# Cross-attention of a decoder layer on one core: batches written out, values copied by ScalarE, their bias added to the heads

## What is computed

```
# query = layernorm(x), (32, 100, 256); key_value = ctx, (32, 361, 192); 16 heads of 16 channels
q = (query @ Wq + bq)   ; k = (key_value @ Wk + bk)   ; v = (key_value @ Wv + bv)   # split into heads
attn = clip(einsum('bhqd,bhkd->bhqk', q, k) * D ** -0.5, -1e4, 1e4)
attn = softmax(attn, axis=-1)
x = einsum('bhqk,bhkd->bqhd', attn, v).reshape(B, Nq, Cq)
return x @ Wo + bo
```

## Time and profile before

| what | value |
|---|---|
| median of three runs | 1663.99 us (1661.3 to 1667.15) |
| the profiled execution | 1657.89 us |
| its span, first to last instruction | 1656.1 us |
| TensorE matmuls busy | 1392.7 us, 84% |
| TensorE weight loads | 973.8 us, 59% |
| VectorE busy | 1054.5 us, 64% |
| ScalarE busy | 516.9 us, 31% |
| GpSimd busy | 785.4 us, 47% |
| mean granted clock of TensorE | 0.926 |

### The profile page before, as it was taken

The page is one execution under the profiler, slowest core; times in us unless marked ns, Lnnn a source line. Parts: engine busy times, 40 slices in busy tenths (PEclk is TensorE's granted clock), DMA queues, the critical chain, the costliest instruction groups (busy, mean ns, idle before and its releaser), DMA issues. The chain is left out here.

```text
span 1656.1 us, 33994 instructions
## 1 busy us (share of the span) xinstructions
PE 1392.7 (84%) x9914; PEld 973.8 (59%) x9915; DVE 1054.5 (64%) x2457; ACT 516.9 (31%) x1228; POOL 785.4 (47%) x1072
## 2 busy tenths in 40 slices
PE   4788778877745998989898898989998499999997
PEld 2556545555533776767676676666765266666664
DVE  2687897788731688868788787878886222222221
ACT  1333323332301334434344343434442122222221
POOL 4233552355332457757576576657774122222222
PEclk9899999999875799989899998999996699999999
DMA  4991000000004545545555454555652122222222
GB/s 144 316 319 31 1 1 1 0 0 1 1 12 84 73 91 108 117 90 111 104 106 109 76 115 103 109 101 102 116 109 62 41 46 45 45 45 45 45 46 25
DMA packets 180315, 128.11 MB, mean 77 GB/s; under 512 B 68882, under 2 KB 173090, under 8 KB 180194
## 3 DMA queue, kind: packets, MB, share of 16 engines
q1 hardware_dynamic: 167890, 112.36, 31.2%
q0 software_dynamic: 12304, 14.10, 5.6%
HBM read 36.23 MB, written 44.83 MB: 49 GB/s over the span
## 5 line engine op out<-in xcount | busy, mean ns | idle before, releaser
L1323 DVE TENSOR_REDUCE neg_raw<-bank_s 100x2 f32<-100x722 f32 x256 | 231.1, 903 | 102.2 <-PE bank_s L1539 102.2
L1225 ACT ACTIVATE prob<-bank_st 120x400 f32<-120x400 f32 (+1 forms) x384 | 166.0, 506 | 270.6 <-PE bank_st L1556 270.6
L1880 POOL DMA_INDIRECT out<-result,target x57 | 88.2, 1547 | 266.9 <-DVE result L1854 263.7
L1334 DVE TENSOR_SCALAR bank_st<-bank_st 120x400 f32<-120x400 f32 (+1 forms) x384 | 196.6, 572 | 0.0
L1539 PE MATMUL bank_s<-k_st,q_st 96*100 96x361 bf16 x512 | 137.3, 352 | 55.7 <-issue 20.7
L1080 POOL TENSOR_TENSOR neg_diag<-xident_b,neg_max 100x400 bf16<-100x400 bf16 x128 | 109.2, 853 | 149.9 <-DVE neg_max L1328 140.9
L748 PE MATMUL bank_l<-q_heads,k 128*100 128x192 f32 (+4 forms) x512 | 126.9, 390 | 62.0 <-DVE attn L562 49.8
L1865 DVE TENSOR_TENSOR hidden<-silu,ebank_v 128x512 f32<-128x512 f32 x57 | 39.2, 687 | 196.1 <-PE ebank_v L1789 196.1
L748 PEld LDWEIGHTS bank_l<-q_heads,k 128*100 128x100 f32 x512 | 82.9, 180 | 112.9 <-DVE attn L562 43.5
L396 ACT ACTIVATE q_heads<-q 32x192 f32<-32x192 f32 (+3 forms) x168 | 62.1, 370 | 226.2 <-DVE q L521 217.8
L1547 PEld LDWEIGHTS bank_st<-q_st,k_st 96*120 96x120 bf16 (+1 forms) x1536 | 117.7, 143 | 12.8 <-ACT prob L1225 0.5
(11 more groups left out here) (203 smaller groups left out, 2688.9 us busy)
## 6 DMA issues: line engine op xcount, KB each, us to landing
k_st<-k_part SPq DMA_DIRECT2D x384, 90.2 KB
slot_rows<-empty SPq DMA_DIRECT2D x9, 2967.0 KB, 26.1
q_st<-q_part SPq DMA_DIRECT2D x384, 25.0 KB
kv<-in_ctx_t SPq DMA_DIRECT2D x32, 270.8 KB
expert_w<-in_w SPq DMA_DIRECT2D x16, 512.0 KB, 3.9
rows<-slot_rows SPq DMA_DIRECT2D x57, 129.0 KB, 2.0
residual<-in_w SPq DMA_DIRECT2D x16, 256.0 KB, 4.1
residual<-in_x SPq DMA_DIRECT2D x8, 400.0 KB
```

The lines of the kernel that those rows point to most:

```text
L1225: act.activation(prob[0:KEYS[c], t % 2, c], bank_st[c][0:KEYS[c], 0:4 * T], ACT.Exp).then_inc(exp_done, 1)
L1323: dve.tensor_reduce(neg_raw[:, h:h + 2], bank_s[0:T, :, 0:S], AX.X, ALU.max, negate=True).then_inc(max_done, 1)
L1334: dve.tensor_scalar(tile, tile, CLAMP, -CLAMP, ALU.min, ALU.max).then_inc(clipped, 1)
```

## The change

Three things. `every_batch` calls `body` for all 32 batches with plain numbers; the counted loop of the attention stage is gone on all five engines. `values`, which moves the value matmuls' results from bank_v to `val`, is now a ScalarE copy without a bias: at t = 0 parts 0 and 1 stand behind `out_copy` and ahead of `exps`, at t = 1 part 2 stands ahead of `heads_turn`. And the bias bv is added where ScalarE copies the turned heads: there the channels lie on partitions, so the bias is one column for each half, and the one copy of 200 columns becomes two instructions of 100 columns with a bias. `out_project` waits for both.

```diff
-def every_batch(eng, body):
-
-    for b in range(4):
-        body(b, b, 0)
-    with eng.Fori(1, BATCH // 4 - 1) as i:
-        for q in range(4):
-            body(4 * i + q, q, i)
-    for b in range(BATCH - 4, BATCH):
-        body(b, b % 4, BATCH // 4 - 1)
+def every_batch(body):
+
+    for b in range(BATCH):
+        body(b, b % 4, b // 4)
...
-        b_v = sb("xb_v", [128, D])
+        b_v = sb("xb_v", [128, CC])
...
             def heads_turn(b):
+
                 act.wait_ge(heads_turned, b + 1)
-                act.activation(heads_t[:], bank_m[:, 0:CC * T].rearrange("p (c t) -> p c t", c=CC),
-                               ACT.Copy).then_inc(heads_t_done, 1)
+                for c in range(CC):
+                    act.activation(heads_t[:, c], bank_m[:, c * T:(c + 1) * T], ACT.Identity,
+                                   bias=b_v[:, c:c + 1]).then_inc(heads_t_done, 1)
+
+            def values(b, p, c):
+                act.wait_ge(v_summed, 3 * b + max(c + 1, 2))
+                act.activation(val[0:KEYS[c], p, c, 0:17 * NH].rearrange("p (h d) -> p h d", d=17)[:, :, 0:16],
+                               bank_v[0:KEYS[c], (c % 2) * D:(c % 2 + 1) * D].rearrange("p (h d) -> p h d", d=16),
+                               ACT.Copy).then_inc(v_done, 1)
...
                 queries(b)
+                if b == 0:
+                    for c in range(3):
+                        values(0, 0, c)
...
                 for t in range(4):
+                    if t == 1 and more_than(b, 1):
+                        values(b + 1, 1 - q % 2, 2)
                     if t == 1 and not first:
                         heads_turn(b - 1)
...
                     if t == 0 and not first:
                         out_copy(b - 1)
+                    if t == 0 and more_than(b, 1):
+                        values(b + 1, 1 - q % 2, 0)
+                        values(b + 1, 1 - q % 2, 1)
...
-            def values(b, p, c):
-                dve.wait_ge(v_summed, 3 * b + max(c + 1, 2))
-                dve.tensor_tensor(val[0:KEYS[c], p, c, 0:17 * NH].rearrange("p (h d) -> p h d", d=17)[:, :, 0:16],
-                                  bank_v[0:KEYS[c], (c % 2) * D:(c % 2 + 1) * D].rearrange("p (h d) -> p h d", d=16),
-                                  b_v[0:KEYS[c], :].rearrange("p (h d) -> p h d", d=16),
-                                  ALU.add).then_inc(v_done, 1)
...
-            for c in range(3):
-                values(0, 0, c)
...
-                    if t == 0 and more:
-                        values(b + 1, 1 - p, 0)
-                        values(b + 1, 1 - p, 1)
-                    if t == 1 and more:
-                        values(b + 1, 1 - p, 2)
...
-                pe.wait_ge(heads_t_done, b + 1)
+                pe.wait_ge(heads_t_done, CC * (b + 1))
...
-        "xbv": np.broadcast_to(a["bv"], (128, D)), "xbo": np.broadcast_to(a["bo"], (T, D)),
+        "xbv": a["bv"].reshape(CC, 128).T, "xbo": np.broadcast_to(a["bo"], (T, D)),
```

More of the change, by code:

```diff
@@ L1020, in body @@
                         load_w2(n - 2)
-            every_batch(sp, body)
+            every_batch(body)
             keep(BATCH - 2)
@@ L1173, in body @@
                     diag(b + 1, 0)
-            every_batch(pool, body)
+            every_batch(body)
             last = BATCH // 2 - 1
@@ L1285, in body @@
                         keys_high(b + 2, t - 2)
-            every_batch(act, body)
+            every_batch(body)
             out_copy(BATCH - 1)
@@ L1471, in body @@
                         negated(n + 1, (t + 1) % 4)
-                    if t == 0 and more:
-                        values(b + 1, 1 - p, 0)
-                        values(b + 1, 1 - p, 1)
-                    if t == 1 and more:
-                        values(b + 1, 1 - p, 2)
-            every_batch(dve, body)
+            every_batch(body)
             last = BATCH // 2 - 1
@@ L1683, in body @@
                             count(2 * i - 1 + q // 2, x_done, b)
-            every_batch(pe, body)
+            every_batch(body)
             last = BATCH // 2 - 1
```

## The result

The changed kernel takes 1612.72 us (median of four runs, 1610.59 to 1614.91); the kernel before took 1665.57 us beside it. The ratio is 0.9675, with a 95% interval of 0.9629 to 0.972: faster by 47 to 62 us. A later comparison on another chip gave 0.9729 (0.9696 to 0.9762), 40 to 51 us. The forecast was 1632 us, 32 us less, with a range that ended at 1616. The side and the main cause were right, the size was some 20 us too small.

A forecast was written before the change was run, and what follows sets the result against it. TensorE, busiest at 84%, was taken to lose time at the attention loop's jumps. Terms -35.9 - 2.8 + 8.1 - 1.0 = -31.6, say -32 us, from 1663.99 gave 1632 us, range 1616 to 1648.

The forecast's parts named there:

- The loop: Attention stage, batches 7 to 24: writing out the counted loop removes five jumps back, 35.9 us saved.
- The wait with "issue": TensorE before a batch's first scores, once per jump back: 20.7 us in all; none over 2.5 us expected after.
- the clock stayed at 1.00: Sign of being right: granted clock 1.00 in every attention pair, with pairs of 43 to 44 us.
- no wait at the pace of the instruction blocks: Gaps at the pace of 16 KB instruction fetches in the attention stage would have shown the prediction wrong.
- The starved rival: Written-out attention code waits for late instruction blocks, up to 1821 us if all 47 are late; chance 0.04.
- VectorE's relief: 96 value additions leave VectorE in the attention batches, 37.6 us of work, almost none on the path: 2.8 us saved.
- The 0.2 us in even batches: Router's MAX8 starts earlier once VectorE's additions go, in 14 even batches with a `place`: 2.8 us saved.
- the late exps: ScalarE copies at t = 0 delay exps 0.4 us; TensorE's wait for `heads` covers it, otherwise 12 us.
- The start: Small parts ahead of batch 0: smaller bias table, batch 0's copies behind `queries(0)`; -0.5 to +1 us, taken as nothing.
- `heads_t`: One ScalarE instruction becomes two with bias, 0.26 us more in 31 batches: 8.1 us added, 1 us taken off.
- The base: Saving applied to the median of three, 1663.99 us; the profiled execution took 1657.89, 6.1 us under it.
- VectorE paces (1612 to 1624): Rival: VectorE sets the pace at t = 1 and t = 2, so shed additions save 13 us more; chance 0.13.

The follow-up runs named there:

- the cover is taken away: Changed kernel with transfers of k and q for slot 5 dropped from batch 2 on: 1605.95 us; also with one-copy heads_t, no bias bv: 1600.49 us.
- the moments first: Kernel before with batches written out and batch 1's moments moved ahead of batch 0's value additions, values and bias staying on VectorE: 1612.39 us.
- the queue blocked on both sides: Changed kernel plus a VectorE wait for batch 0's value copies before batch 1's moments, 1625.21 us; beside kernel before with only the loop written out, 1619.18 us.
- slot 5 left out: Four of 24 spreading transfers dropped from batch 2 on: 1594.83 us written out, moments first, additions on VectorE; 1605.95 us in the changed kernel.
- the run with one line moved: Kernel before, loop kept, with VectorE's moments of batch 1 moved ahead of batch 0's three value additions: 1642.8 us, ratio 0.9931.

## Why the prediction was right and wrong

- **The loop.** 35.9 us forecast for nine pairs; in the same 18 batches the written-out kernel saves 34.9 us (428.10 - 393.16), over 31 batches 34.2, and by the medians 32 to 42. Right, in mechanism, place and size, as far as one profiled execution of a looped kernel can tell. The wait with "issue" went, the clock stayed at 1.00, no wait at the pace of the instruction blocks came: between 540 and 1200 us the changed kernel fetches 53 blocks of 16 KB and 40 of 8 KB, against 61 and 11 before, and the pairs don't feel it. The starved rival fell. That the gap of a jump is the fetch of its target is read from the earlier trace rows and from the 8 large blocks that went with the loop; no run takes it apart from the rest of the jump.
- **The values.** That VectorE's relief is worth little in the batches was right, and the kernel with only that part shows nothing at all there (428.09). The 0.2 us in even batches did not come out. That the late exps are covered by the wait for `heads` was right: t = 0 grew by 0.17 us and not by 0.4, and the wait for `heads` shrank.
- **The start.** This is the step that failed: "the copies of batch 0 wait behind `queries(0)` on ScalarE. Between -0.5 and +1 us". I looked at where the copies went and not at what had stood behind the additions that left. It was worth 9.0 us in the start, and with it batch 0 became 3.8 us shorter, by the clock. The row that would have told it was in the trace of before: GpSimd's longest single wait of the stage, the 9.68 us for xmean_var.
- **`heads_t`.** +8.1 us forecast with 1 us of cover; 3.0 us where the cover is taken away, and nothing to be told from scatter where it is there. The instruction pair did grow by about what the row of `qf` said, and the wait doubled. What I mis-sized is the cover: I took the wait for q_st as it stood before, in twelve batches (12.1 us), but once the jumps are gone it stands in 18 batches of the changed kernel and in 20 of the one that is only written out (13.5 and 18.4 us), and then anything shorter than that wait is free.
- **The base.** The profiled execution of before lay 6 us under its median and had a mixer stage of 494.0 us; the changed kernel's had 488.9. 5 of the 46 us between the two spans are scatter of an untouched stage. I had given the runs of one kernel no such spread in the range.
- **The agreement in the batches is in part luck.** 31.6 us forecast, 32.4 measured. Beside the loop the forecast had -2.8 us for VectorE's relief, which did not come, and +7.1 for the bias (8.1 less 1.0), most of which is covered: +4.3 together. What came is +3.6 for all that moved, with one batch in it that alone is 5.0 us longer and that the prediction does not have (see below), and -1.8 by the queue, inside the batches.
- **The rival that the number would favour.** 1612.72 us lies at the lower end of "VectorE paces (1612 to 1624)". Its mechanism is not what happened: the kernel with only the values and the bias moved gains nothing in batches 1 to 30, and the one with VectorE's work as before is as fast as the changed one.

Step by step from one profile to the next, start and 31 batches together: the loop written out, -34.1 us; the moments first, -11.0 (-9.2 in the start, -1.8 in the batches); the copies and the bias moved, +3.7. That makes -41.4 us. It lies in the interval of the second comparison (40 to 51 us) and, with the 5.1 us of the mixer stage, at the edge of the first (47 to 62). The last two terms are the loose ones: with the repeated profile of the changed kernel the copies cost 7.8 us, and with the queue blocked on both sides 0.3.

## One pair that stays long

In the changed kernel and in every other one with the copies on ScalarE and the loop written out, and in none with the additions, batch 12 takes 25 to 27 us. The timeline of the changed kernel there:

```profile
786.48 2.15 DVE L1401 TENSOR_TENSOR slots<-slot_f,first_slot 100x4 uint32<-100x4 f32 x1
...
786.91 0.88 POOL L1056 TENSOR_TENSOR kr<-kf,k_part 128x361 f32<-128x361 f32 x1
787.74 0.87 POOL L1057 TENSOR_TENSOR k_part<-kf,k_part 128x361 bf16<-128x361 f32 x1
...
788.55 0.90 DVE L1327 TENSOR_REDUCE neg_raw<-bank_s 100x2 f32<-100x722 f32 x1
...
789.50 0.51 PE L1536 MATMUL bank_s<-k_st,q_st 96*100 96x361 bf16 x2 [1.63 <-DVE neg_raw L1327]
```

An instruction of four elements a row, 0.16 us elsewhere (median 163 ns), takes 2.15 us; two GpSimd instructions of 0.88 us on SBUF lie inside it. TensorE waits 1.63 us, and the granted clock falls to 0.5 for the next 10 us. The trace of before has the same thing on a small scale: in 7 of its 16 cases this instruction (L1397 there) starts while GpSimd's `neg_diag` (L1080) has some 0.26 us to go, and then it takes 0.27 to 0.29 us and ends with it; where 0.13 us or less is left, it takes 0.16. In batch 12 here 0.47 us is left, and it ends with the second GpSimd instruction behind that one, at 788.63 and 788.61 us. That fits an instruction held up by GpSimd's; that the two meet in SBUF is not shown, it was not tried by itself, and why it starts so early just in batch 12 stays open. It costs 4 to 5 us, of the 10.4 that the copies cost with slot 5 left out half.

## What to carry over

When work leaves an engine's queue, look at what stood behind it, above all in the few instructions ahead of a steady state: a wait for something not needed can hold up a whole chain, and the order of one line may be worth as much as the move. A wait ahead of a dense stretch can also cost inside it: here batch 0 ran at the lower clock for longer, 3.8 us, of which some came back later. The jump of this loop cost its gap and then a stretch at half clock, and both are read off by comparing passes with and without one. A saving or a cost on the busiest engine can vanish in another queue's wait: take that wait away before judging either, and look in which batches the gain then lies.

## What the hardware showed beyond expectation

- A jump back of the loop cost 4.1 us of gap and some 3 us more at 1.2 GHz and behind it: 7.0 us in all for each of five, in the profiled execution; in that of the run with one line moved the five pairs took 8 us more.
- Starting a transfer of q or k costs SyncE's queue about 0.6 us (median 591 ns for those of k), so 24 of them fill some 15 of the 21.8 us of a batch; four of them cost ScalarE 2.54 us in a gap that it had.
- After a start with TensorE's scores late by 9 us the granted clock stayed at 0.5 into the third step of batch 0: 24.4 to 25.6 us for the batch, 19.8 to 20.5 in the other kernels.
- The same mixer code took 488.9 to 496.0 us over 14 executions on several chips; the kernel before took 1643 to 1678 us. With such a spread only stage times, not totals, tell a few microseconds.
